# A two-half selective-scan block: output projection, second softplus and row norm moved

## The chip, the cores and the metric

The kernel runs on one core of a Trainium2 chip. Time is device time in microseconds (us) of one execution. Engines are named as in the profile: PE is TensorE's matrix multiply and PEld its weight load, DVE is VectorE, ACT ScalarE, POOL GpSimd, SP the engine that issues most transfers. The engines run side by side and wait for each other on semaphores; each runs its own instructions strictly in the order written.

## The reference, cut to what matters

Four sequences (batches) of 512 tokens with 128 channels pass a Mamba block with a mixture of experts, a feed-forward block, an attention and a feed-forward block. The change touches the Mamba block alone and the norm behind it:

```
xi, z = split(x @ in_proj_w)                 # 256 channels each
xi    = silu(causal_conv(xi) + conv_b)
dbc   = xi @ x_proj_w                        # 64 dt columns, 16 B, 16 C
delta = softplus(dbc[:, :64] @ dt_proj_w + dt_proj_b)
for n in 16 states:                          # scan over the 512 tokens
    h = exp(delta * A[n]) * h + (delta * xi) * B[n]
    y += h * C[n]
y = (y + D_skip * xi) * silu(z)
r = residual + y @ out_proj_w
h2 = r * rsqrt(mean(r * r) + eps) * w2       # then router, top 2 of 8 experts
```

## The kernel before, in words

Channels lie on the 128 partitions (256 channels are CT = 2 tiles) and tokens along the free dimension. The four batches are worked in two halves h = 0, 1 of HB = 2 batches each (c = 0, 1). In each batch the NS = 16 states are numbered on through g = 16 * (2h + c) + n, so the first half has states 0 to 31, the second 32 to 63.

**A state's work.** For each g, ScalarE writes the two decays `exp(delta * A)` into PSUM banks 6 and 7 (`decay`, L1061), each behind the scan of the state before that reads the same bank. GpSimd forms dBx (L850) from dx = delta * xc (L840 for c = 0, L855 for c = 1) and a row of B that SP has spread over all partitions, up to three states ahead. VectorE scans each tile (`scan`, L1387) and weighs the state by its row of C (`weigh`, L1397), for which ScalarE has copied that row into a bank (`copy_c`, L1057). Some states (1, 3, 6, 8, 11, 13 of a batch, in the last batch only 5 and 10) are weighed by GpSimd (L862) and have neither `weigh` nor `copy_c`. TensorE sums y in banks 0 and 1 by products with the identity (`ysum`). VectorE's order is scan(g, 0), weigh(g - 1), scan(g, 1). At the end of a batch `gate` multiplies by silu(z).

**The start of a half.** TensorE: `x_proj` of a batch (two products of 512 columns) and, once ScalarE has copied the result to SBUF (`row_copy`, L980), `dt_proj` (two more, banks 2, 3 for c = 0 and 4, 5 for c = 1). SP stores the copied B and C rows to DRAM and spreads them from there. ScalarE makes the softplus: `relu_abs` (Abs and Relu of each tile, L985 and L986) and `exp_log` (Exp, Ln over both tiles, L990 and L991). VectorE adds the two parts (`form_delta`, L1340), which sets the semaphore `s_dl` for GpSimd's dx and ScalarE's decays. In the first half the order is, on ScalarE, both row copies, the table load, then softplus of batch 0 and of batch 1, and on TensorE both x products, then both dt products. The scans start after both.

**The end of the first half.** `out_proj(0)` projects the gated y of the first half (32 matmul records, banks 0 and 1). It stands last in the second half's `inputs_1`, after both dt products. VectorE then adds it to the residual (`add_residual`, L1347), takes the moments for the norm, and GpSimd raises them to the power -1/2. This stands between form_delta(2) and form_delta(3), so ahead of all scans of the second half. `h2_norm(0)` multiplies the eight 128x128 tiles of the first half by their factors on VectorE (L1364), after the scans of state 35; TensorE transposes them at g = 36, ScalarE copies them out with w2 at g = 38 (`moe_input`, L957), then come router (39), logits (41), top (42), exp (43), second top part (44), rank (45) and slots (47), all woven between states by the table `ROUTE_AT`. From state 48 on GpSimd sends one `scatter` (L827) of normalised rows behind each dBx, sixteen in all. Similar tables (`COPY_AT`, `PREP_AT`) weave other copies into the first half.

## Time and profile before

| | us |
|---|---|
| median of 3 runs | 712.5 (711.13 to 716.41) |
| the profiled execution | 713.09 |
| its span in the trace | 711.1 |
| mean granted TensorE clock | 0.932 |
| busy: PE, DVE, ACT, POOL | 564.9, 495.1, 386.8, 329.6 |

The scans of the first half run from 48 to 147 us, those of the second from 175 to 291 us. Then come the mixture of experts with the first feed-forward block worked in, and the attention. A busy time counts instructions of an engine, not whether anything waits for them. In the timelines a row with "x8" is eight instructions of one kind that follow each other, with the time from the first one's start to the last one's end; in brackets stands the idle time of the engine before it and who ended it. PEclk is the granted clock of TensorE as a share of 2.4 GHz.

### The profile page before, as it was taken

What the parts mean: (1) busy time and instruction counts of PE and PEld (TensorE: products, weight loads), DVE (VectorE), ACT (ScalarE), POOL (GpSimd) and SP (SyncE); (2) the same over time, 40 slices, a digit from 0 to 9 for tenths busy, and PEclk for the clock granted to TensorE, in tenths of its full rate; (3) what the DMA queues carried; (4) which work ended last, traced back from release to release, by engine and by line L of the source; (5) the groups of instructions that cost most, each with busy time, mean ns of one, the idle gap of its engine ahead of it and who ended that gap; (6) DMA issues with size and microseconds to landing.
All of it is one profiled execution on the core that took longest, in us unless ns stands there. A gap on an engine that the chain in (4) does not pass through costs nothing.

```text
span 711.1 us, 11057 instructions
## 1 busy us (share of the span) xinstructions
PE 564.9 (79%) x3447; PEld 356.1 (50%) x3447; DVE 495.1 (70%) x1304; ACT 386.8 (54%) x610; POOL 329.6 (46%) x287
## 2 busy tenths in 40 slices
PE   3939789584585766688999899966789989989887
PEld 1314333232241222387999799932545545545366
DVE  5649999976999998634533565388787778887052
ACT  1586655575364445366766556623256566566741
POOL 5259989815788799232678332433012103112010
PEclk9978999988688988999999999976999999999999
DMA  5836555404566566030114200422103003000001
GB/s 148 282 124 189 152 177 157 154 26 152 178 179 205 170 166 167 18 88 12 46 54 120 86 20 24 116 82 77 39 2 105 10 3 107 3 3 1 2 16 46
DMA packets 50523, 65.91 MB, mean 93 GB/s; under 512 B 7730, under 2 KB 29250, under 8 KB 50210
## 3 DMA queue, kind: packets, MB, share of 16 engines
q1 hardware_dynamic: 45122, 59.27, 28.8%
q0 software_dynamic: 2496, 5.15, 2.0%
q10 hardware_dynamic: 2848, 0.78, 0.5%
q8 instruction: 29, 0.48, 0.3%
q14 instruction: 28, 0.23, 0.1%
HBM read 47.46 MB, written 9.52 MB: 80 GB/s over the span
## 4 chain that ended last, share of the span: by engine, by line
PE 32%; DVE 9%; issue 8%; POOL 5%; ACT 4%; ACTq 1%; DMA 0%; POOLq 0%; DVEq 0%
PE ps L1594 29%; DVE arena L1514 3%; POOL moe_out L835 2%; ACT arena L1129 2%; POOL moe_rows L827 1%; PE ps L1891 1%; DVE x L1449 1%; DVE nb L1228 1%; DVE stats L1215 1%; POOL arena L878 1%; ACT r L1129 1%; PE ps L1898 1%; ACT arena L1137 1%; ACT arena L1149 0%; ACTq L1119 0%
## 5 line engine op out<-in xcount | busy, mean ns | idle before, releaser
L1594 PE MATMUL ps<-arena 128*128 128x128 f32 (+11 forms) x2150 | 326.0, 328 | 41.1 <-DVE arena L1514 17.5
L1594 PEld LDWEIGHTS ps<-arena 128*128 128x128 f32 (+2 forms) x2150 | 207.4, 158 | 126.8 <-issue 55.6
L1594 PE MATMUL ps<-arena,ident 128*128 128x512 f32 x256 | 137.7, 681 | 67.2 <-DVE arena L1397 67.1
L1387 DVE TENSOR_TENSOR_SCAN arena<-ps,arena 128x512 f32<-128x512 f32 x128 | 149.0, 1205 | 7.8 <-ACT ps L1061 4.2
L1061 ACT ACTIVATE ps<-arena 128x512 f32<-128x512 f32 x128 | 87.7, 691 | 91.7 <-DVE arena L1387 91.5
L850 POOL TENSOR_TENSOR arena<-arena 128x1024 f32<-128x1024 f32 x64 | 127.1, 2004 | 7.2 <-DVE arena L1387 6.6
L1514 DVE CUSTOM_DVE_ANT_0 arena<-ps,cmask 128x128 f32<-128x128 f32 (+3 forms) x256 | 111.5, 487 | 26.4 <-PE ps L1594 26.0
L1594 PEld LDWEIGHTS ps<-arena,ident 128*128 128x128 f32 x256 | 52.8, 217 | 147.2 <-DVE arena L1397 91.8
L835 POOL DMA_INDIRECT moe_out<-arena,xT x46 | 44.9, 976 | 69.9 <-DVE arena L1538 57.4
L1129 ACT ACTIVATE arena<-ps 128x1024 f32<-128x1024 f32 (+3 forms) x86 | 57.1, 709 | 36.0 <-PE ps L1594 35.6
L1568 DVE TENSOR_TENSOR arena<-arena,ps 128x512 f32<-128x512 f32 x46 | 31.6, 687 | 63.9 <-PE ps L1594 46.5
L1175 ACT COPY arena<-arena 128x1024 f32 x46 | 48.2, 1047 | 23.6 <-issue 14.0
L807 POOL TENSOR_TENSOR small<-small,neghalf 128x4 f32<-128x4 f32 (+1 forms) x14 | 15.6, 1114 | 89.2 <-DVE small L1465 73.9
L1397 DVE TENSOR_TENSOR arena<-arena,ps 128x1024 f32<-128x1024 f32 x44 | 52.6, 1195 | 0.2
L862 POOL TENSOR_TENSOR arena<-arena 128x1024 f32<-128x1024 f32 x20 | 47.2, 2359 | 11.2 <-DVE arena L1387 10.5
L1185 ACT ACTIVATE arena<-ps 128x512 f32<-128x512 f32 x52 | 31.1, 598 | 24.0 <-PE ps L1594 22.5
L891 POOL TENSOR_TENSOR x<-x,arena 128x128 f32<-128x128 f32 x16 | 7.4, 461 | 67.4 <-DVE arena L1527 67.2
L827 POOL DMA_INDIRECT moe_rows<-nb,xT x32 | 32.2, 1008 | 13.3 <-issue 7.0
L1129 ACT ACTIVATE r<-ps 128x512 f32<-128x512 f32 (+3 forms) x42 | 27.8, 701 | 17.1 <-PE ps L1594 16.7
L1594 PE MATMUL ps<-kmask,identb 128*128 128x128 bf16 x256 | 35.1, 219 | 0.0
L1548 DVE TENSOR_TENSOR arena<-arena,ps 128x512 f32<-128x512 f32 x18 | 12.3, 684 | 27.1 <-ACT arena L1149 27.0
L1594 PEld LDWEIGHTS ps<-kmask,identb 128*128 128x128 bf16 x256 | 23.7, 98 | 12.4
(198 smaller groups left out, 621.3 us busy)
## 6 DMA issues: line engine op xcount, KB each, us to landing
arena<-bc_rows SPq DMA_DIRECT2D x128, 256.0 KB, 3.8
arena<-arena SPq DMA_DIRECT2D x64, 64.0 KB
arena<-arena SPq DMA_DIRECT2D x28, 128.0 KB, 2.5
moe_rows<-arena SPq DMA_DIRECT2D x2, 1495.0 KB, 11.7
arena<-moe_rows SPq DMA_DIRECT2D x8, 325.0 KB, 4.7
arena<-in_L_attn_a_Wg SPq DMA_DIRECT2D x8, 256.0 KB, 4.5
arena<-in_L_attn_a_Wu SPq DMA_DIRECT2D x8, 256.0 KB, 5.0
arena<-moe_out SPq DMA_DIRECT2D x4, 512.0 KB, 4.9
```

The lines of the kernel that those rows point to most:

```text
L827: G.indirect_dma_start(moe_rows[h], bass.IndirectOffsetOnAxis(ap=slotu[:, h, k, t:t + 1], axis=0), nbr[:, t // TB, t % TB, :], None).then_ ...
L835: G.indirect_dma_start(moe_out[h], bass.IndirectOffsetOnAxis(ap=target[:, h, k:k + 1], axis=0), yb[:, i % YR, :], None).then_inc(s_yst[i % ...
L850: G.tensor_tensor(dBx[:, g % RING, :, :], dx[:, :, cs], bs[:, g % BS, :].unsqueeze(1).to_broadcast([P, CT, L]), ALU.mult).then_inc(s_dbx, 1)
L862: G.tensor_tensor(hC[:, k % SUMS, :, :], hst[:, p % STATES, :, :], cs_rows[:, p % CS, :].unsqueeze(1).to_broadcast([P, CT, L]), ALU.mult). ...
L1061: S.activation(bank(6 + e), delta[:, e, c * L:c * L + L], ACT.Exp, scale=aneg[:, e, n:n + 1]).then_inc(s_da, 1)
L1129: S.activation(pts[c % 3][:, 2 * q:2 * q + 2, kt * P:L], ps[:, 2 * q:2 * q + 2, kt * P:L], ACT.Exp).then_inc(s_ex, 1)
L1175: S.copy(wst[:, i % 2, :, :].rearrange("p g f -> p (g f)"), wgu[:, bass.ds(expert, 1), :, :].rearrange("p o g f -> p (o g f)")).then_inc(s ...
L1387: V.tensor_tensor_scan(hst[:, g % STATES, e, :], bank(6 + e), dBx[:, g % RING, e, :], 0.0, ALU.mult, ALU.add).then_inc(s_scan, 1)
L1397: V.tensor_tensor(hC[:, k % SUMS, :, :], hst[:, g % STATES, :, :], bank(2 + dve_count(g) % 2).unsqueeze(1).to_broadcast([P, CT, L]), ALU.m ...
L1514: last = V.tensor_tensor_reduce(out=junk[:, m % 2, col:col + w], in0=ps[:, 4 + m % 2, col:col + w], in1=cmask[:, L - w:L], scale=-1.0, sca ...
L1568: V.tensor_tensor(hs[:, i % 2, :], sg[:, m % 2, :], bank(2 + m % 2), ALU.mult).then_inc(s_hm, 1)
L1594: return T.matmul(o, l, rr, start=start, stop=stop)
```

## The change

Seven edits, all at the two starts of the halves and at the routing of the first half:

- TensorE, first half: dt_proj(0, c) follows x_proj(0, c) batch by batch.
- TensorE, second half: out_proj(0) stands behind dt_proj(1, 0), ahead of x_proj(1, 1).
- ScalarE, both halves: row copy, Abs and Relu, Exp and Ln of batch 1 stand behind the decays and the C copy of the half's first state.
- VectorE, both halves: form_delta of batch 1 stands behind the scans of the half's first state; the weighing of that state waits for it.
- VectorE, second half: add_residual(0) stands ahead of form_delta(2), the moments behind it, and both ahead of the first scan.
- ScalarE has the first half's norm (`norm_h2`), four tiles behind state 35 and four behind state 36.
- The rest of the routing is one state later, and so are the scatters, with two behind the last state.

```diff
-        ROUTE_AT = {"h2norm": first_1 + 3, "h2turn": first_1 + 4, "input": first_1 + 6, "router": first_1 + 7,
+        NORM_AT = (first_1 + 3, first_1 + 4)
+        ROUTE_AT = {"h2turn": first_1 + 5, "input": first_1 + 7, "router": first_1 + 8,
...
-                        j = c * NS + n - NS
-                        if h and 0 <= j < 2 * TH:
+                        j = c * NS + n - NS - 1
+                        if h and 0 <= j < 2 * TH - 1:
                             scatter(0, j // 2, j % 2)
+                        if h and j == 2 * TH - 2:
+                            scatter(0, TH - 1, 1)
...
+            def norm_h2(c):
+
+                act.wait_ge(s_rstd, 3)
+                for j in range(TB):
+                    t = TB * c + j
+                    last = S.activation(nb[:, c, j, :], r[:, t, :], ACT.Copy, scale=small[:, 2, t:t + 1])
+                last.then_inc(s_h2, 1)
...
-                for c in range(HB):
-                    row_copy(0, c)
+                row_copy(0, 0)
                 S.preload_act_table_set("natural_log_exp_and_others")
-                for c in range(HB):
-                    relu_abs(0, c)
-                    exp_log(c)
+                relu_abs(0, 0)
+                exp_log(0)
...
                 relu_abs(1, 0)
-                row_copy(1, 1)
                 exp_log(0)
-                relu_abs(1, 1)
-                exp_log(1)
...
+                        if c == n == 0:
+                            row_copy(h, 1)
+                            relu_abs(h, 1)
+                            exp_log(1)
+                        if g in NORM_AT:
+                            norm_h2(g - NORM_AT[0])
...
-                    for b in range(HB):
-                        form_delta(b)
+                    form_delta(0)
                 else:
+                    add_residual(0)
                     form_delta(HB)
-                    add_residual(0)
-                    form_delta(HB + 1)
+                    residual_moments(0)
...
+                    if g == state_of(HB * h, 0):
+                        dve.wait_ge(s_dl, HB * h + HB)
...
-                        if g == ROUTE_AT["h2norm"]:
-                            h2_norm(0, count["var"])
+                        if c == n == 0:
+                            form_delta(HB * h + 1)
...
                     x_proj(0, c)
-                for c in range(HB):
                     dt_proj(0, c)
...
                 dt_proj(1, 0)
+                out_proj(0)
                 pe.wait_ge(s_xc, 2 * HB + 4)
                 pe.wait_ge(s_zc, 2 * HB)
                 x_proj(1, 1)
                 dt_proj(1, 1)
-                out_proj(0)
```

The order of instructions, first on ScalarE at the start of the first half, before (L980 is the row copy, L985 and L986 are Abs and Relu, L990 and L991 Exp and Ln, L1061 the decays, L1057 the C copy):

```order
L980 COPY arena<-ps 96x512 [waits x_proj_done] x2
L1012 ACT_TABLE_LOAD
L985 ACTIVATE arena<-ps,arena 128x512 [waits dt_proj_done]
...
L990 ACTIVATE arena<-arena 128x1024 [waits act_chain]
L991 ACTIVATE arena<-arena 128x1024 [waits act_chain]
L985 ACTIVATE arena<-ps,arena 128x512 [waits dt_proj_done]
...
L990 ACTIVATE arena<-arena 128x1024 [waits act_chain]
L991 ACTIVATE arena<-arena 128x1024 [waits act_chain]
L1061 ACTIVATE ps<-arena 128x512 [waits delta_ready]
```

and now (L991 is the row copy, L996 and L997 are Abs and Relu, L1001 and L1002 Exp and Ln, L1067 the decays, L1063 the C copy):

```order
L991 COPY arena<-ps 96x512 [waits x_proj_done]
L1022 ACT_TABLE_LOAD
L996 ACTIVATE arena<-ps,arena 128x512 [waits dt_proj_done]
...
L1001 ACTIVATE arena<-arena 128x1024 [waits act_chain]
L1002 ACTIVATE arena<-arena 128x1024 [waits act_chain]
L1067 ACTIVATE ps<-arena 128x512 [waits delta_ready]
L1067 ACTIVATE ps<-arena 128x512
L1063 COPY ps<-arena 128x512 [waits c_row_spread0]
L991 COPY arena<-ps 96x512 [waits x_proj_done]
L996 ACTIVATE arena<-ps,arena 128x512 [waits dt_proj_done]
...
L1002 ACTIVATE arena<-arena 128x1024 [waits act_chain]
L1067 ACTIVATE ps<-arena 128x512 [waits scan_done] x4
```

The second row copy and softplus have moved behind the first state's decays and C copy; the row copy and the dt product that answers it now stand between them and that softplus.

VectorE at the start of the second half, before (L1340 is the delta add, L1347 the residual add, L1215 the first step of the moments, L1387 the scan, L1397 the weighing):

```order
L1340 TENSOR_TENSOR arena<-ps,arena 128x2x512 [waits softplus_log_ready]
L1347 TENSOR_TENSOR r<-ps,r 128x512 [waits out_proj_done] x2
L1215 BN_STATS stats<-r 128x6 [waits residual_ready]
...
L1340 TENSOR_TENSOR arena<-ps,arena 128x2x512 [waits softplus_log_ready]
L1387 SCALAR_TENSOR_TENSOR arena<-ps,arena 128x512 [waits hC_on_pool_ready,dBx_ready,dA_ready]
```

and now (L1352 is the delta add, L1359 the residual add, L1227 the moments, L1400 the scan, L1412 the weighing):

```order
L1359 TENSOR_TENSOR r<-ps,r 128x512 [waits out_proj_done] x2
L1352 TENSOR_TENSOR arena<-ps,arena 128x2x512 [waits softplus_log_ready]
L1227 BN_STATS stats<-r 128x6 [waits residual_ready]
...
L1400 SCALAR_TENSOR_TENSOR arena<-ps,arena 128x512 [waits hC_on_pool_ready,dBx_ready,dA_ready]
L1400 SCALAR_TENSOR_TENSOR arena<-ps,arena 128x512 [waits dA_ready]
L1352 TENSOR_TENSOR arena<-ps,arena 128x2x512 [waits softplus_log_ready]
L1400 SCALAR_TENSOR_TENSOR arena<-ps,arena 128x512 [waits hC_ready,dBx_ready,dA_ready]
L1412 TENSOR_TENSOR arena<-arena,ps 128x1024 [waits y_summed,delta_ready,scan_done,c_row_copied]
```

The residual adds have gone ahead of the first delta add, and the second delta add has gone behind the scans of state 32.

ScalarE around states 35 to 39, now (L986 is the norm, L960 the copy with w2; before, no norm stood here and the copy with w2, L957, stood one state earlier, behind decays with no C copy):

```order
L1067 ACTIVATE ps<-arena 128x512 [waits scan_done] x2
L986 ACTIVATE nb<-r,small 128x128 [waits rstd_ready]
L986 ACTIVATE nb<-r,small 128x128 x3
L1067 ACTIVATE ps<-arena 128x512 [waits scan_done] x2
L1063 COPY ps<-arena 128x512 [waits hC_ready,c_row_spread0]
L986 ACTIVATE nb<-r,small 128x128 [waits rstd_ready]
L986 ACTIVATE nb<-r,small 128x128 x3
L1067 ACTIVATE ps<-arena 128x512 [waits scan_done] x2
L1063 COPY ps<-arena 128x512 [waits hC_ready,c_row_spread1]
L1067 ACTIVATE ps<-arena 128x512 [waits scan_done] x4
L1063 COPY ps<-arena 128x512 [waits hC_ready,c_row_spread0]
L960 ACTIVATE arena<-ps,w2c 128x512 [waits h2_transposed] x2
```

The norm stands behind the decays of state 35 and behind the C copy of state 36, the copy with w2 behind the C copy of state 39.

## Rows read from the trace of the kernel before

**Rows 1.** The chain that ended last, from 280 to 305 us: start us, us, what.
```profile
296.36 3.85 PE ps L1594 x32
```

**Rows 2.** Windows, two scan loops: busy (x) of PE, PEld, DVE, ACT, POOL; PEclk, DMA.
```profile
48.00:147.40 99.40, 78.20 (x178) 32.33 (x179) 95.21 (x84) 61.57 (x112) 90.91 (x44) 0.93 0.53 159
174.70:291.70 117.00, 76.94 (x160) 31.40 (x161) 112.57 (x143) 56.44 (x90) 95.57 (x55) 0.81 0.59 172
```

**Rows 3.** Timeline, VectorE, first half's start: start, us, engine, operation, [idle before <-releaser].
```profile
42.12 1.23 DVE L1340 TENSOR_TENSOR arena<-ps,arena 128x1024 f32<-128x1024 f32 x1 [9.29 <-ACT arena L991]
46.47 1.23 DVE L1340 TENSOR_TENSOR arena<-ps,arena 128x1024 f32<-128x1024 f32 x1 [3.12 <-ACT arena L991]
47.96 3.45 DVE L1387 TENSOR_TENSOR_SCAN arena<-ps,arena 128x512 f32<-128x512 f32 x3 [0.27 <-POOL arena L850]
```

**Rows 4.** Timeline, ScalarE, first half's start.
```profile
34.02 0.58 ACT L980 COPY arena<-ps 96x512 f32<-96x512 f32 x1 [0.44 <-PE ps L1594]
...
36.34 1.28 ACT L1012 ACT_TABLE_LOAD   x1
37.63 0.69 ACT L985 ACTIVATE arena<-ps,arena 128x512 f32<-128x512 f32 x1
```

**Rows 5.** Windows (us, PE busy (x), PEclk), then timeline, of TensorE at either clock.
```profile
41.00:42.00 1.00, 0.24 (x1) 1.00 0.15 55
...
45.00:46.00 1.00, 0.00 (x0) 0.50 0.00 0
...
158.00:159.00 1.00, 1.00 (x2) 0.50 0.71 160
...
155.51 1.98 PE L1594 MATMUL ps<-arena 64*128 64x512 f32 x4 [1.21 <-ACT arena L980]
...
179.27 3.78 PE L1594 MATMUL ps<-arena,ident 128*128 128x512 f32 x4 [9.05 <-DVE arena L1397]
```

**Rows 6.** Timeline, VectorE, second half's start.
```profile
163.73 1.23 DVE L1340 TENSOR_TENSOR arena<-ps,arena 128x1024 f32<-128x1024 f32 x1 [8.37 <-ACT arena L991]
...
167.50 0.69 DVE L1347 TENSOR_TENSOR r<-ps,r 128x512 f32<-128x512 f32 x1 [1.09 <-PE ps L1594]
168.22 1.65 DVE L1215 BATCH_NORM_STATS2 stats<-r 128x6 f32<-128x128 f32 x8
...
173.53 1.22 DVE L1340 TENSOR_TENSOR arena<-ps,arena 128x1024 f32<-128x1024 f32 x1
174.67 3.44 DVE L1387 TENSOR_TENSOR_SCAN arena<-ps,arena 128x512 f32<-128x512 f32 x3
```

**Rows 7.** Timeline, VectorE: the norm of the first half's rows, and the second half's.
```profile
185.86 6.22 DVE L1364 TENSOR_SCALAR nb<-r,small 128x128 f32<-128x128 f32 x8
...
308.97 1.65 DVE L1364 TENSOR_SCALAR nb<-r,small 128x128 f32<-128x128 f32 x8
```

**Rows 8.** Timeline, ScalarE, then VectorE, then ScalarE: copies between two states' decays.
```profile
75.73 0.42 ACT L967 CAST wuT<-ps 128x128 fp32r<-128x128 f32 x2
...
76.83 1.34 ACT L1061 ACTIVATE ps<-arena 128x512 f32<-128x512 f32 x2
...
77.60 1.22 DVE L1387 TENSOR_TENSOR_SCAN arena<-ps,arena 128x512 f32<-128x512 f32 x1 [0.81 <-ACT ps L1061]
...
198.35 1.25 ACT L957 ACTIVATE arena<-ps,w2c 128x512 f32<-128x512 f32 x2
```

**Rows 9.** Groups by form, ScalarE; then waits, 20 to 300 us (total us, times, longest).
```profile
L1162 ACT ACTIVATE arena<-ps,w2c 128x128 f32<-128x128 f32 x46 | 16.9, 367 | 19.6 <-PE ps L1781 19.6
...
ACT ps L1057 <- DMA arena<-bc_rows: 8.1, 10, 1.6
```

**Rows 10.** Timeline, GpSimd then VectorE, second half's last 16 states.
```profile
235.00 1.22 POOL L827 DMA_INDIRECT moe_rows<-nb,xT  x1 [4.07 <-DVE xT L1317]
...
288.01 1.01 POOL L827 DMA_INDIRECT moe_rows<-nb,xT  x1 [0.17 <-issue]
...
281.51 1.22 DVE L1387 TENSOR_TENSOR_SCAN arena<-ps,arena 128x512 f32<-128x512 f32 x1 [2.05 <-issue]
```

9 lines of the change are left out of this document (5 added, 4 removed).

## The prediction

> **What bounds the kernel now.** I read the windows over the two scan loops first. In the first loop VectorE is busy 95.2 of 99.4 us, in the second 112.6 of 117.0; ScalarE is busy about half of either, GpSimd 90.9 and 95.6 [rows 2]. So inside the loops time is won or lost on VectorE's stream, and a ScalarE instruction costs something only where it makes a decay late. Next I read the timelines at the two places where VectorE has no scan to do: the start of either half. In the first, VectorE waits 9.29 us for the softplus of batch 0, adds it (42.12), waits 3.12 us for batch 1's, adds that (46.47), and its first scan (47.96) waits 0.27 us more for GpSimd [rows 3]. In the second it waits 8.37 us, forms delta at 163.73, then takes the residual add, moments and the second delta (173.53) before its first scan at 174.67 [rows 6]. Last I read the chain from 280 us on: from the last scan it goes through the output projection (32 matmul records in 3.85 us, 296.36 to 300.21) into the mixture of experts [rows 1]. Everything after 300 us is unchanged and should shift as a block.
>
> **First half: the first scan earlier, the second state later.** Now TensorE runs batch 0's dt product ahead of batch 1's x product, and ScalarE has one row copy instead of two before its table load. The copy ends at 34.60, the load takes 1.28, so the first Abs can start at 35.9 instead of 37.63 [rows 4]. From that Abs to the delta add is 42.12 - 37.63 = 4.49 us, so the add comes at 40.4, and the first scan, 47.96 - 42.12 = 5.84 us behind it (GpSimd's two products), at 46.2: 1.7 us earlier. But state 1 now needs more. weigh of state 0 and the scans of state 1 stand behind the delta add of batch 1, and that behind ScalarE's: two decays (a pair takes 1.34 us [rows 8]), a C copy, the row copy of batch 1 (0.58), and a round trip to TensorE. The decays start when batch 0's delta is there, 41.65; the row copy ends at about 44.1. TensorE has by then stood still since about 38.5: batch 0's dt product from 34.65 and batch 1's x product, each as four records of 512 columns at 1.98 us [rows 5]. Before, its granted clock was still 1.00 in 41 to 42, where its work ended, and 0.50 (1.2 of 2.4 GHz) in 45 to 46 [rows 5]. The gap is now nearly 6 us, so I take the product at the lower level: four records of 512 columns took 1.98 us at the upper level and 3.78 at the lower [rows 5]. The two outputs are then there at 46.0 and 47.9; of the 4.49 us softplus, 1.14 precede the second Abs, so it ends at 47.9 + 3.35 = 51.25 and state 1's scan starts at 52.4. Before it started 2.24 us behind 47.96, at 50.2 (three scans in 3.45 us are 1.12 apart [rows 3]). **Term 1: +2.2 us**; at the upper clock 45.1 + 4.49 gives a scan at 50.8, +0.6.
>
> **Second half: the residual work into the wait.** out_proj(0) moves ahead of batch 1's x product on TensorE. It can start when dt_proj(1, 0) ends, 155.51 + 1.98 = 157.5 [rows 5]. The granted clock was 0.50 in 158 to 159 [rows 5], and TensorE's work up to 157.5 is the same, so I let the dip recur to 161: at 0.24 us a record (double of 3.85/32 [rows 1]) the first 16 records end at 161.3, the others at 163.2. VectorE adds the two residuals (0.69 each [rows 6]) at 161.3 and 163.2, and only then, being in order, forms batch 0's delta: at 163.9, no earlier than before (163.73 [rows 6]), though its softplus is ready at 161.3. GpSimd's products and the decays are queued behind that. Then come the moments: 173.53 - 168.22 = 5.3 us [rows 6], to 170.4; GpSimd's first dBx is there at 169.5. States of batch 0 start at 170.4. ScalarE meanwhile: decays at 165.1, C copy, row copy, done 167.4; dt product at the upper clock, first output 168.45, softplus to 172.95, delta to 174.15. Scan of state 33 at 174.15 against 174.67 + 2.24 = 176.9. **Term 2: -2.75 us.** With no clock dip in the output projection it is -4.5; with the dt product at the lower clock too, -0.9.
>
> **The norm.** The eight multiplications stop VectorE between two scans for 6.15 us (6.22, of which some 0.1 overlaps the next scan); the same eight take 1.65 us at 308.97 [rows 7]. The difference is that GpSimd is busy at 185.86. What leaves the path here is the 6.15 that it measures there. Is GpSimd then the next bound? It is busy 95.6 of 117.0 us in this loop [rows 2], so taking 6.2 us from the loop still leaves it over 15 us idle. **Term 3: -6.15 us.** The Trainium skill, SBUF — State Buffer, SBUF: two separate sides, says that a two-port VectorE form and GpSimd lock each other out for a whole instruction while ScalarE has ports of its own; the 6.22 against 1.65 us agree with it.
>
> **What ScalarE pays.** Its four multiplications for batch 0 fall behind state 35's decays, where no C copy stands; slack covers them. The other four come behind state 36's C copy, and state 35 is GpSimd's, so VectorE has no weighing to do between the scans that the next decay must catch. The same pattern stands in the first half: four small copies and one large one between 75.73 and 76.83 (1.10 us) made VectorE wait 0.81 [rows 8]. A 128x128 ACTIVATE of this kind takes 367 ns [rows 9]; started in a row I take 0.2 to 0.25 us apart, so four are 1.0 us and the stall 0.75. The two w2 copies (1.25 us [rows 8]) move from state 38, which had no C copy, to 39, which has one and follows a GpSimd state: by the same pattern 0.85; and they now wait for transposes that TensorE runs behind one more sum (3.78 us at the lower clock), so 0.95. **Term 4: +1.7 us**, 0.8 to 3. Bounds: nothing if the slack were as at the old places, twice 1.2 if none. The Trainium skill, ScalarE: Activation LUTs, What ACT_TABLE_LOAD costs, prices such an ACTIVATE at 386 ns with 93 ns of overlap; by it four take an estimated 1.27 us and the sum would be 0.25 us higher.
>
> **The rest.** The routing chain (logits, top, rank, slots) sits one state later throughout, and the first scatter too. GpSimd waited 4.07 us for the slots before it, then ran without a gap, and VectorE waited for it (2.05 us at 281.51 [rows 10]). It now starts one state of VectorE later (3.36 us) with one step of 3.2 us less to do before that point: **term 5: +0.1 us**. The sixteenth scatter moves behind GpSimd's last dBx; the fifteenth and sixteenth end about 290, the projection that gates the loads ends at 300.2 [rows 1, 10], so 10 us cover them; without that cover it would cost about 1 us. SP's store of batch 1's rows now waits for the later row copy, up to 44.1; behind it is the B row of state 3, which waits for GpSimd's first product (about 46) anyway. Sum: 2.2 - 2.75 - 6.15 + 1.7 + 0.1 = -4.9 us, from the profiled execution's 713.09 (span 711.1) to 708.2. That execution lies 0.6 above the median 712.5, so on its basis **707.6 us**, within 1% (about what a measurement of this kernel can tell from no change).
>
> **Rivals.**
> 1. *The clock stays up* at both places. Against it: the rows at 0.50; for it: the dip in the second half came while TensorE was at work, so a shift of 2 us may move it. Terms 1 and 2 become +0.6 and -4.5, which gives 704.2. Chance 0.2.
> 2. *Transfers and copies hold ScalarE.* Ten C copies waited 8.1 us in all for their row, the longest 1.6 [rows 9]. The pause of 6 us in which rows and expert weights arrived is gone, so three more such waits of about 1 us may surface as late decays: 710.6. Chance 0.18.
> 3. *GpSimd becomes the bound* when the pause goes. It decides if GpSimd's work from the norm to the slots is longer than VectorE's; then term 3 is worth nothing, and 2.2 - 2.75 + 1.7 + 0.1 = +1.25 gives 713.7: slower than before. The idle share in [rows 2] speaks against it. Chance 0.05.
> The forecast itself, 705.8 to 709.5, has 0.57.
>
> **How the numbers follow.** The range reaches from rival 1 to a little past rival 2: 704.0 to 711.2, which leaves out part of rival 1 and rival 3. Faster by over 1% is below 705.4: rival 1 and the forecast's edge, 0.25. Slower by over 1% (above 719.6) needs more than any rival gives: 0.02. The rest, 0.73, is within 1%.
>
> **What would show it.** In the changed profile: first scan at about 46.2 and VectorE waiting some 2.7 us for the Ln before batch 1's delta; the second dt product of the first half at clock 0.50. In the second half residual adds ahead of the delta, that delta near 166.1 (163.9 + 2.2), and state 33's scan near 176.4 (174.15 + 2.2). No VectorE tensor_scalar between states 35 and 36, and two waits for ScalarE of 0.7 to 1 us before states 37 and 40. The last projection near 295.5 instead of 300.2. I am wrong if the second delta of either half is not bound by ScalarE, if GpSimd ends the waits between 180 and 230 us, or if the block behind 300 us changes its length by over 1 us.

## The result

| us | before | changed |
|---|---|---|
| median of 22 runs each | 713.22 (711.13 to 716.41) | 710.55 (706.68 to 714.67) |
| ratio to before, 95% | | 0.9962 (0.9946 to 0.9977) |
| the profiled execution | 713.09 | 710.80 |
| its span | 711.1 | 709.0 |
| mean granted TensorE clock | 0.932 | 0.915 |
| busy: PE, DVE, ACT, POOL | 564.9, 495.1, 386.8, 329.6 | 576.2, 487.1, 389.4, 328.9 |

The change is worth 2.7 us by the medians (1.6 to 3.9 by the interval of the ratio), with 4.9 forecast. The times of all tables are us. PE is busy 11.3 us longer in this pair though its matmuls are the same: the mean granted clock was 0.915 against 0.932.

### The start of the first half

The timeline of the changed kernel, VectorE, 40 to 54 us (start, us, engine, line, operation, [idle before <-releaser]); it answers to [rows 3]:

```profile
40.79 1.23 DVE L1352 TENSOR_TENSOR arena<-ps,arena 128x1024 f32<-128x1024 f32 x1 [7.58 <-ACT arena L1002]
46.62 2.34 DVE L1400 TENSOR_TENSOR_SCAN arena<-ps,arena 128x512 f32<-128x512 f32 x2 [4.60 <-POOL arena L851]
51.58 1.23 DVE L1352 TENSOR_TENSOR arena<-ps,arena 128x1024 f32<-128x1024 f32 x1 [2.62 <-ACT arena L1002]
52.72 1.21 DVE L1400 TENSOR_TENSOR_SCAN arena<-ps,arena 128x512 f32<-128x512 f32 x1
```

ScalarE in the same place, and the clock of TensorE in two windows (us, busy (xinstructions) of PE, PEld, DVE, ACT, POOL, then PEclk, DMA share, GB/s); they answer to [rows 4, 5]:

```profile
43.80 0.57 ACT L991 COPY arena<-ps 96x512 f32<-96x512 f32 x1
46.54 0.69 ACT L996 ACTIVATE arena<-ps,arena 128x512 f32<-128x512 f32 x1 [2.16 <-PE ps L1610]
...
48.24 0.69 ACT L996 ACTIVATE arena<-ps,arena 128x512 f32<-128x512 f32 x1 [0.47 <-PE ps L1610]
...
42.00:43.00 1.00, 0.00 (x0) 0.00 (x0) 0.02 (x1) 0.95 (x2) 0.90 (x1) 0.61 0.00 0
43.00:52.00 9.00, 7.49 (x8) 2.33 (x8) 2.76 (x3) 6.34 (x10) 8.92 (x5) 0.50 0.38 105
```

The first scan comes 1.3 us earlier than before (46.62 against 47.96), state 1's scan 2.5 us later (52.72 against 50.2). What is late is batch 1's softplus: TensorE had stood still for 5.5 us when the row copy ended at 44.37, the clock had fallen to 0.50 in 42 to 43, and the dt product's two outputs let ScalarE start at 46.54 and, after 0.47 us more of waiting, at 48.24.

### The start of the second half

VectorE of the changed kernel, 161 to 176 us, beside [rows 6]; then the TensorE clock in two windows:

```profile
161.51 0.69 DVE L1359 TENSOR_TENSOR r<-ps,r 128x512 f32<-128x512 f32 x1 [4.14 <-PE ps L1610]
163.30 0.69 DVE L1359 TENSOR_TENSOR r<-ps,r 128x512 f32<-128x512 f32 x1 [1.09 <-PE ps L1610]
163.90 1.22 DVE L1352 TENSOR_TENSOR arena<-ps,arena 128x1024 f32<-128x1024 f32 x1
...
169.72 2.34 DVE L1400 TENSOR_TENSOR_SCAN arena<-ps,arena 128x512 f32<-128x512 f32 x2
173.75 1.23 DVE L1352 TENSOR_TENSOR arena<-ps,arena 128x1024 f32<-128x1024 f32 x1 [1.69 <-ACT arena L1002]
174.89 1.21 DVE L1400 TENSOR_TENSOR_SCAN arena<-ps,arena 128x512 f32<-128x512 f32 x1
...
158.00:162.00 4.00, 4.00 (x27) 2.96 (x26) 0.49 (x1) 3.99 (x6) 0.00 (x0) 1.00 0.44 120
...
169.00:173.00 4.00, 4.00 (x5) 1.17 (x4) 3.00 (x3) 3.50 (x6) 4.00 (x3) 0.50 0.47 116
```

The residual adds stand in what was a wait, as intended. The clock fell in another place than forecast: the projection (158 to 162) ran at 1.00, and in 169 to 173, where batch 1's dt product runs, it was 0.50. State 33's scan starts at 174.89. The first half ended 2.0 us later than before (the convolution's first multiplication on VectorE at 150.63, before at 148.63), so counted from there state 33 gained 4.0 us.

### What ScalarE's four copies and the routing cost

The eight norm copies on ScalarE (two rows), with the copy of a C row, the w2 copies and the logits copy further on:

```profile
181.24 1.26 ACT L986 ACTIVATE nb<-r,small 128x128 f32<-128x128 f32 x4
...
185.11 1.27 ACT L986 ACTIVATE nb<-r,small 128x128 f32<-128x128 f32 x4
...
195.44 0.59 ACT L1063 COPY ps<-arena 128x512 f32<-128x512 f32 x1 [0.89 <-DMA arena<-bc_rows]
195.97 1.26 ACT L960 ACTIVATE arena<-ps,w2c 128x512 f32<-128x512 f32 x2
...
207.27 0.21 ACT L974 COPY wtok<-ps 128x64 f32<-128x64 f32 x1 [2.49 <-PE ps L1610]
```

and the three scans on VectorE that waited for a decay behind them, with the router product on TensorE and its clock:

```profile
186.99 1.22 DVE L1400 TENSOR_TENSOR_SCAN arena<-ps,arena 128x512 f32<-128x512 f32 x1 [0.82 <-ACT ps L1067]
...
197.84 1.22 DVE L1400 TENSOR_TENSOR_SCAN arena<-ps,arena 128x512 f32<-128x512 f32 x1 [1.79 <-ACT ps L1067]
...
208.10 1.23 DVE L1400 TENSOR_TENSOR_SCAN arena<-ps,arena 128x512 f32<-128x512 f32 x1 [1.20 <-ACT ps L1067]
...
203.81 3.42 PE L1610 MATMUL ps<-rw,arena 128*128 128x8 f32 x16
...
200.00:208.00 8.00, 7.77 (x21) 5.26 (x22) 6.90 (x7) 3.75 (x8) 6.78 (x5) 0.50 0.64 216
```

Before, no scan between 174 and 238 us waited for ScalarE by over 0.3 us. Now they wait 0.82 + 1.79 + 1.20 = 3.81 us, where term 4 had 1.7. The second wait is a C row that came 0.89 us late by DMA, with 1.26 us of w2 copies behind it in front of the decays. In all six profiled executions of this kernel the second wait is 0.90 us plus the lateness of that row: the row is 0.25, 0.80, 0.86, 0.89, 0.91 or 1.61 us late, the scan waits 1.15, 1.70, 1.76, 1.79, 1.80 or 2.51 us. So the w2 copies by themselves cost the 0.9 that I had put down, and the row is what comes on top. Why the row is late no run shows.

The third wait I had costed at nothing: the copy of the logits now stands one state on, and waited 2.49 us for the router's sixteen products, which took 3.42 us at the lower clock; the decays are queued behind it. The other executions bear this out: in the second the clock was back at 1.00 from 202.3 us on, the products took 1.85 us and no scan waited there; in the five others they took 3.42 us and the scan waited 1.20 or 1.21.

A fourth wait for ScalarE, of 1.64 us at 257.83 (1.13 to 1.17 us at that state in the kernel before), costs nothing: from the first scatter to the last scan GpSimd sets the pace, with 0.30 us of idle time or less between its rows, and that stretch takes 52.2 us in all six.

### Behind 300 us

The chain that ended last, 280 to 300 us, of the changed kernel (start, us, what), for [rows 1]:

```profile
291.04 3.85 PE ps L1610 x32
```

The last projection ends at 294.89, before at 300.21: 5.3 us earlier, with 295.5 forecast. So the profiled execution has the whole forecast gain there, and 709.04 - 294.89 = 414.15 us behind it, against 410.86: 3.3 us were lost in a block that the change does not touch. Chains of both kernels run in step from there to 488 us; then two pieces in the attention differ. The changed kernel, and the kernel before at the second of them:

```profile
488.84 2.91 PE ps L1610 x10
...
509.05 4.59 PE ps L1610 x24
```

```profile
494.08 1.14 PE ps L1594 x8
...
512.73 2.96 PE ps L1594 x24
```

The clock in the changed kernel's windows is 0.50 in both pieces:

```profile
488.00:492.00 4.00, 3.77 (x14) 3.00 (x14) 2.07 (x11) 2.68 (x3) 2.22 (x3) 0.50 0.34 92
...
510.00:513.00 3.00, 3.00 (x16) 3.00 (x15) 0.00 (x0) 0.00 (x0) 0.00 (x0) 0.50 0.14 16
```

Two questions follow: which term was mis-sized, and whether the loss in the attention belongs to the change. The comparison of one profiled execution with one other can't answer either, so twelve of the runs below are the two kernels again. "Theory C" in the expectations is that the clock falls there by chance, whatever the kernel; theory B is that the change brings it.

### The profile page after: what moved, and what is told of

It is laid out like the page before. It is cut to its first block, busy times and chain, and to the rows that moved or that the text cites. A ratio compares the mean times of both kernels' runs of the same rounds, so it can differ in the third digit from the quotient of the medians.

```text
span 709.0 us, 11038 instructions
## 1 busy us (share of the span) xinstructions
PE 576.2 (81%) x3428; PEld 364.3 (51%) x3447; DVE 487.1 (69%) x1296; ACT 389.4 (55%) x618; POOL 328.9 (46%) x287
## 4 chain that ended last, share of the span: by engine, by line
PE 33%; DVE 9%; issue 7%; POOL 4%; ACT 4%; DMA 1%; ACTq 1%; POOLq 0%; another core or an unknown queue 0%; DVEq 0%; SPq 0%
PE ps L1610 30%; DVE arena L1530 3%; POOL moe_out L836 2%; ACT arena L1141 2%; POOL moe_rows L828 1%; DVE x L1465 1%; PE ps L1906 1%; DVE stats L1227 1%; POOL arena L881 1%; DVE nb L1240 1%; ACT r L1141 1%; PE ps L1913 1%; DMA arena<-moe_out 1%; ACT arena L1161 1%; ACT arena L1149 1%
## 5 line engine op out<-in xcount | busy, mean ns | idle before, releaser
L1610 PE MATMUL ps<-arena 128*128 128x128 f32 (+10 forms) x2131 | 328.8, 331 | 50.2 <-DVE arena L1530 17.9
L1610 PEld LDWEIGHTS ps<-arena 128*128 128x128 f32 (+2 forms) x2150 | 209.8, 159 | 135.9 <-issue 56.0
L1610 PE MATMUL ps<-arena,ident 128*128 128x512 f32 x256 | 140.2, 693 | 46.6 <-DVE arena L1412 46.5
L1400 DVE TENSOR_TENSOR_SCAN arena<-ps,arena 128x512 f32<-128x512 f32 x128 | 149.3, 1208 | 15.8 <-ACT ps L1067 8.0
L1067 ACT ACTIVATE ps<-arena 128x512 f32<-128x512 f32 x128 | 87.3, 690 | 81.2 <-DVE arena L1400 78.0
L1187 ACT COPY arena<-arena 128x1024 f32 x46 | 48.2, 1047 | 23.9 <-issue 14.5
L1412 DVE TENSOR_TENSOR arena<-arena,ps 128x1024 f32<-128x1024 f32 x44 | 52.7, 1198 | 0.2
L1063 ACT COPY ps<-arena 128x512 f32<-128x512 f32 x44 | 25.4, 577 | 8.6 <-DMA arena<-bc_rows 8.6
## 6 DMA issues: line engine op xcount, KB each, us to landing
arena<-bc_rows SPq DMA_DIRECT2D x128, 256.0 KB, 3.8
arena<-in_L_attn_a_Wg SPq DMA_DIRECT2D x8, 256.0 KB, 4.4
arena<-in_L_attn_a_Wu SPq DMA_DIRECT2D x8, 256.0 KB, 5.0
```

What stands on the lines that cost most here:

```text
L1067: S.activation(bank(6 + e), delta[:, e, c * L:c * L + L], ACT.Exp, scale=aneg[:, e, n:n + 1]).then_inc(s_da, 1)
L1187: S.copy(wst[:, i % 2, :, :].rearrange("p g f -> p (g f)"), wgu[:, bass.ds(expert, 1), :, :].rearrange("p o g f -> p (o g f)")).then_inc(s ...
L1400: V.tensor_tensor_scan(hst[:, g % STATES, e, :], bank(6 + e), dBx[:, g % RING, e, :], 0.0, ALU.mult, ALU.add).then_inc(s_scan, 1)
L1412: V.tensor_tensor(hC[:, k % SUMS, :, :], hst[:, g % STATES, :, :], bank(2 + dve_count(g) % 2).unsqueeze(1).to_broadcast([P, CT, L]), ALU.m ...
L1610: return T.matmul(o, l, rr, start=start, stop=stop)
```

## Experiments: one part at a time

Each diff is against the changed kernel. The first four runs share one chip, with 713.31 us for the kernel before (29 runs).

**The first half's start as before.**

```diff
-                row_copy(0, 0)
+                for c in range(HB):
+                    row_copy(0, c)
...
-                        if c == n == 0:
+                        if h and c == n == 0:
                             row_copy(h, 1)
...
-                    form_delta(0)
+                    for b in range(HB):
+                        form_delta(b)
...
                     x_proj(0, c)
+                for c in range(HB):
                     dt_proj(0, c)
```

> The changed kernel with the start of the first half as it was before: both row copies and both softpluses ahead of the first scan, both x products ahead of the dt products. Theory A (terms add up): this undoes the loss that the trace of the changed kernel shows there (state 1's scan 52.72 instead of 50.2 us), so the last output projection ends 2.0 to 2.5 us earlier than in the changed kernel, at about 292.6, and the time is 2 to 2.5 us below the changed kernel's median of 710.6. Theory B (what is gained ahead of 300 us is given back behind it, because the block behind starts earlier): the projection ends as early, but the whole is within 0.7 us of the changed kernel.

Measured: 708.61 us, ratio 0.9922 (0.9904 to 0.9941), 6 runs. By the medians that is 1.8 us faster than the changed kernel on the same chip (710.42, ratio 0.9959), by the ratios 2.6. So the first half's edit costs time, about what was expected of it. The profiled execution does not show it at the projection, which ends at 295.1 and not at the expected 292.6: its first half started late, with the granted clock at 0.50 from 33.4 to 36.8 us, and its stretch from state 33 to the last scan took 111.7 us. The section on the repeated executions sorts this out.

**The norm on VectorE again.** The rest of the change stays; routing and scatters stand at their old states.

```diff
-        NORM_AT = (first_1 + 3, first_1 + 4)
+        NORM_AT = ()
+        ROUTE_AT = {"h2norm": first_1 + 3, "h2turn": first_1 + 4, "input": first_1 + 6, "router": first_1 + 7,
+                    "logits": first_1 + 9, "top_a": first_1 + 10, "exp": first_1 + 11, "top_b": first_1 + 12,
+                    "rank": first_1 + 13, "slots": first_1 + 15}
...
+                        if g == ROUTE_AT["h2norm"]:
+                            h2_norm(0, 3)
```

> The changed kernel with the norm of the first half's rows back on VectorE behind state 35, and with it the routing and the scatters at their old states. Theory A: VectorE has its 6.2 us again and loses the three waits for ScalarE and the router (0.82, 1.79 and 1.20 us at 187, 198 and 208 us), so the last projection ends 2.0 to 2.8 us later than in the changed kernel, at about 297.3, and the time is up by as much. If the forecast's price for ScalarE (1.7 us) had been right it would be 4.4 us later. Theory B: later by 2 to 3 us at the projection, but the whole within 1 us of the changed kernel.

Measured: 714.08 us, ratio 1.0000 (0.9981 to 1.0019), 12 runs: 3.7 us over the changed kernel. VectorE, where the norm stands:

```profile
186.48 6.22 DVE L1377 TENSOR_SCALAR nb<-r,small 128x128 f32<-128x128 f32 x8
```

The price of the norm on VectorE is what it was (6.22, as in [rows 7]). I had expected 2.0 to 2.8 us and got 3.7 by the medians; by the ratios (1.0000 against 0.9959) it is 2.9, and the intervals do not rule out the forecast's 6.15 - 1.7. The trace is sharper: from state 33's scan to the last scan it takes 113.52 us, as in the kernel before, against 110.5 on average in the changed kernel, so the norm's move with all that it brings is worth 3.0. Without the norm's move the change brings nothing.

**The second half's start as before.**

```diff
+                row_copy(1, 1)
                 exp_log(0)
+                relu_abs(1, 1)
+                exp_log(1)
...
                 else:
-                    add_residual(0)
                     form_delta(HB)
+                    add_residual(0)
                     residual_moments(0)
+                    form_delta(HB + 1)
...
                 dt_proj(1, 0)
-                out_proj(0)
                 pe.wait_ge(s_xc, 2 * HB + 4)
...
                 dt_proj(1, 1)
+                out_proj(0)
```

> The changed kernel with the start of the second half as it was before: output projection last on TensorE, residual work between the two delta adds, both softpluses ahead of the first scan. Theory A: the last projection ends 2.5 to 4 us later than in the changed kernel (2.75 was the forecast's term with the clock at its lower level during the projection, 4.0 is what the two traces show), and the time is up by as much, to about 713 to 714. Theory B: the whole stays within 1 us of the changed kernel's.

Measured: 711.92 us, ratio 0.9983 (0.9967 to 1.0000), 12 runs: 1.5 us over the changed kernel, with 2.5 to 4 expected. The intervals of the two overlap (0.9938 to 0.9980 for the changed kernel), so the sign is likely and the size is rough. In its profile state 33's scan comes 26.66 us behind the end of the first half; in the changed kernel this is 24.26 in the first profile and 24.85 on average, so on average the second half's edit is worth 1.8 there. Together the three parts give +1.8 - 3.7 - 1.5 = -3.4 us, with -2.9 measured for the whole.

**The changed kernel again, and the kernel before again** (the second in a later series on the same chip, like the three runs behind it, with 713.71 us for the kernel before, 20 runs).

> The changed kernel again, for a second profile and as the yardstick of the three others. Theory C (the block behind 300 us varies with where TensorE's clock falls, whatever the kernel): it was 410.9 us long before and 414.1 us in the changed kernel's first profile; a second profile gives another value, anywhere from 410 to 415. Theory B: about 414 again. The last projection ends within 1 us of 294.9 unless the clock falls elsewhere in the first 200 us, which can move it by up to 2 us.

> The kernel before again, for a second profile and as a null comparison. Theory C (the clock moves both parts from one execution to the next, whatever the kernel): the last projection does not end at 300.2 us again and the block behind it is not 410.9 us long again; so far five profiles of the changed kernel and its variants gave 412.0 to 414.2, so about 412.5 is expected here too, with the projection ending between 298.5 and 301. Theory B (the block behind is longer because of the change): 410.9 us again, within 0.5. The ratio is 1.000 within 0.002.

Measured: 710.42 us, ratio 0.9959 (0.9938 to 0.9980), and 712.33 us, ratio 0.9991 (0.9968 to 1.0015). The medians repeat. Behind 300 us the changed kernel's second profile has 412.0 us (414.15 in the first) and that of the kernel before 410.6 (410.86): the latter is what theory B had expected, and I had expected 412.5 by theory C. The profile of the kernel before does not repeat, however, at the place that term 2 was read from. Here it is beside [rows 6], with the clock windows at the same place of this run and then of the first profile:

```profile
162.24 1.23 DVE L1340 TENSOR_TENSOR arena<-ps,arena 128x1024 f32<-128x1024 f32 x1 [6.76 <-ACT arena L991]
...
173.17 3.44 DVE L1387 TENSOR_TENSOR_SCAN arena<-ps,arena 128x512 f32<-128x512 f32 x3
...
159.00:160.00 1.00, 0.49 (x2) 0.00 (x0) 0.00 (x0) 0.70 (x2) 0.00 (x0) 1.00 0.93 240
```

```profile
159.00:160.00 1.00, 1.00 (x3) 0.28 (x1) 0.00 (x0) 0.17 (x1) 0.00 (x0) 0.50 0.78 225
```

The same kernel has the clock at 1.00 there, forms delta 1.5 us earlier and has its scan at 173.17 instead of 174.67. The dip on which I built term 2 was a matter of that one execution.

**TensorE kept busy ahead of the late dt products.** Small products into a bank that is free then.

```diff
+            def keep_warm(n):
+                for _ in range(n):
+                    mm(ps[:, 4, 0:P], ident[:], opw[:, 0, :])
...
                     x_proj(0, c)
+                    if c:
+                        keep_warm(20)
                     dt_proj(0, c)
...
                 x_proj(1, 1)
+                keep_warm(9)
                 dt_proj(1, 1)
```

> The changed kernel with 20 small products (128x128, operands already there, result overwritten) on TensorE ahead of batch 1's dt product in the first half and 9 in the second, to fill the time in which it waits for the row copy. If the lower clock is what makes that product late (two outputs 1.7 us apart in both halves of the changed kernel's profile instead of about 1), the granted clock stays at 1.00 there, the product takes 2.0 us instead of 3.4 to 3.8, and state 1's and state 33's scans come about 1.5 us earlier each: time down by up to 3 us against the changed kernel. If it is the row copy and the softplus themselves, nothing changes (within 0.5 us).

Measured: 708.03 us, ratio 0.9904 (0.9871 to 0.9937), 6 runs. ScalarE in its second half, then the clock in both places:

```profile
169.81 0.69 ACT L996 ACTIVATE arena<-ps,arena 128x512 f32<-128x512 f32 x1 [1.21 <-PE ps L1610]
...
170.97 0.69 ACT L996 ACTIVATE arena<-ps,arena 128x512 f32<-128x512 f32 x1
...
44.00:48.00 4.00, 4.00 (x37) 3.88 (x36) 0.22 (x1) 2.33 (x4) 3.62 (x2) 1.00 0.10 23
...
168.00:171.00 3.00, 2.46 (x6) 0.97 (x6) 2.84 (x12) 1.79 (x5) 2.92 (x3) 1.00 0.09 22
```

The clock stays at 1.00 and the wait of 0.47 us ahead of the second Abs is gone. But in the first half the twenty products stand in front of the dt product and hold it: ScalarE waited 2.42 us for it, where the changed kernel waited 2.16. State 1's scan came at 54.63 in this profile, because the clock was low from 33 to 43 us already; in the two executions of the changed kernel with such an early fall it came at 54.09 and 54.39. State 33's scan came 24.00 us behind the end of the first half, against 24.26. So its profile shows 0.3 us in the second half and nothing in the first, where I had expected 1.5 us each. By the medians the kernel is 2.4 us better than the changed one, by the ratios (0.9904 against 0.9959) 3.9. I can't account for that from the trace; with 6 runs and an interval of 4.7 us part of it may be chance.

**Norm copies and routing copies in the gaps.** The second four norm copies go one state on, behind the C copy of state 37, whose scans follow a weighing. Turn, input and router go one state on too, so the w2 copies come to state 40, which has no C copy.

```diff
-        NORM_AT = (first_1 + 3, first_1 + 4)
-        ROUTE_AT = {"h2turn": first_1 + 5, "input": first_1 + 7, "router": first_1 + 8,
+        NORM_AT = (first_1 + 3, first_1 + 5)
+        ROUTE_AT = {"h2turn": first_1 + 6, "input": first_1 + 8, "router": first_1 + 9,
```

> The changed kernel with the second four tiles of the norm one state later (behind state 37, two scans that follow a weighing), the transposes behind it, and the two w2 copies at state 40, which has no C copy, with the router at 41. Theory A: the waits of VectorE for ScalarE of 0.82, 1.79 and 1.20 us in the changed kernel go, all but about 0.5 us, so the time is 3 us lower than the changed kernel's. Rival: the time is bound there by something else that then shows (the C rows' transfers, or the router), and less than 1.5 us comes.

Measured: 708.03 us, ratio 0.9914 (0.9885 to 0.9943), 6 runs: by the ratios (0.9914 against 0.9959) 3.2 us better than the changed kernel, by the medians 2.4. The waits that are left:

```profile
191.24 1.23 DVE L1400 TENSOR_TENSOR_SCAN arena<-ps,arena 128x512 f32<-128x512 f32 x1 [0.85 <-ACT ps L1067]
...
207.18 1.22 DVE L1400 TENSOR_TENSOR_SCAN arena<-ps,arena 128x512 f32<-128x512 f32 x1 [1.29 <-ACT ps L1067]
```

2.14 us instead of 3.81, where I had expected about 0.5 to be left. The wait at the w2 copies is gone; the one behind the norm copies has only moved to state 38, and the one behind the logits copy (state 43) is 1.29 though the router's products took 1.84 us there; in both places a C row came over 1 us late (1.07 and 1.05). From state 33's scan to the last scan it takes 109.05 us, the changed kernel 110.5 on average: that is the 1.4 us of it that the trace shows. ScalarE's price depends on which gap a copy stands in, and the sum over the waits ahead of the first scatter is where it is read.

**The best of these: copies in the gaps, first half as before.** Both diffs above in one kernel.

> The same placement of norm, copies and router as in e7, and the start of the first half as before the change (as in e1, which was 1.8 us under the changed kernel). If the parts add up: 4.5 to 5 us below the changed kernel, at about 706.

Measured: 706.80 us, ratio 0.9918 (0.9892 to 0.9944), 9 runs. Its median is the lowest of all and near the expected 706, but its ratio is that of the run before it, so by the times the two can't be told apart (in its profile the last projection ends at 291.26, in that run's at 294.46); against the changed kernel both are better by the ratios (0.9914 and 0.9918 against 0.9959), with intervals that just overlap. One wait of 1.23 us for ScalarE is left between state 33 and the first scatter (scan at 189.88), and the span of its profiled execution is 702.9.

## Experiments: the same two kernels, again and again

To tell the change from the execution, both kernels were profiled on more occasions, one execution each, without an edit. The chips of these runs take some 10 us longer in the mixture of experts, so whole times are compared only within a chip; the stretches ahead of 300 us and the attention agree between chips.

> The kernel before, one more profile. In its two profiles the block from the last expert input (456.8 and 454.3 us) to the end of the span was 254.3 and 254.9 us long; in seven of the eight profiles of the changed kernel and its variants it was 257.2 to 257.6, with a drop of TensorE's granted clock some 58 us behind the last expert input that the kernel before did not show. Theory C (where the clock falls in that block is chance, whatever the kernel): a further profile of the kernel before shows the drop and about 257 in more than half of the cases. Theory B (the change brings it): 254 to 255 again and no drop.

> As the look before: theory C wants about 257 us behind the last expert input in one or both of the two, theory B 254 to 255 in both.

> The changed kernel, a third profile. Theory C: the block behind the last expert input lies anywhere from 254 to 258 us; theory B: 257 to 257.6 again. The last projection ended at 294.9 and 293.5 in the two profiles so far; the spread over the first 300 us comes from the clock during the dt products and the output projection of the two starts, so 293 to 297.

> As the look before. With four profiles of either kernel the mean end of the last projection should be about 5 us earlier in the changed kernel if the sum of the forecast holds for the first 300 us, or about 3 if the difference of the medians (2.9 us) is already made there.

> The kernel before, once more. The stretch from the last expert input copy to the end took 254.3, 254.9, 254.8 and 257.2 us in its four profiled executions, and 254.8 to 257.5 in the changed kernel's four, the long value with a low-clock stretch some 57 us behind the copy. Theory C (where the clock falls in the attention is chance, with the same odds for both kernels): of the four looks of the kernel before that are taken now, about two or more show 257. Theory B (the change makes the fall likely): at most one of the four does. End of the first half near 148.6, state 33's scan 26.7 behind it.

> As the fifth look of the kernel before: theory C gives about two or more long attention parts (257 us) in four looks, theory B at most one.

> As the fifth look of the kernel before: theory C gives about two or more long attention parts (257 us) in four looks, theory B at most one.

> The changed kernel once more. Both theories: 33rd state's scan 24.3 us behind the end of the first half, last projection 3 to 5 us earlier than in the kernel before on the same chip. Theory B expects the attention part near 257 us in nearly every look of this kernel; theory C in some two of three.

> As the fifth look of the kernel before: theory C gives about two or more long attention parts (257 us) in four looks, theory B at most one.

> As the fifth look of the changed kernel: theory B expects the attention part near 257 us in nearly every look of this kernel, theory C in some two of three.

Lengths of the stretches, each from its first row in VectorE's timeline, the projection's row in the chain, and the last expert's input copy on ScalarE:

| execution | start to end of first half | from there to state 33's scan | from there to the last scan | last projection ends at | last expert input to the end | span |
|---|---|---|---|---|---|---|
| before, first | 148.63 | 28.28 | 113.57 | 300.21 | 254.3 | 711.1 |
| before, second | 148.75 | 26.66 | 113.50 | 298.65 | 254.9 | 709.2 |
| before, third | 147.90 | 26.66 | 113.50 | 297.80 | 254.8 | 719.8 |
| before, fourth | 149.19 | 26.67 | 113.51 | 299.11 | 257.3 | 724.2 |
| before, fifth | 147.42 | 26.66 | 113.49 | 297.30 | 257.5 | 723.0 |
| before, sixth | 147.27 | 26.65 | 113.50 | 297.16 | 257.5 | 725.2 |
| before, seventh | 149.30 | 26.66 | 113.57 | 299.26 | 255.3 | 723.2 |
| before, eighth | 149.48 | 26.66 | 113.51 | 299.39 | 256.0 | 724.6 |
| changed, first | 150.63 | 24.26 | 110.26 | 294.89 | 257.5 | 709.0 |
| changed, second | 149.75 | 24.39 | 109.63 | 293.51 | 257.2 | 705.5 |
| changed, third | 152.10 | 24.26 | 110.23 | 296.33 | 257.3 | 720.0 |
| changed, fourth | 149.39 | 26.09 | 112.30 | 297.52 | 254.8 | 719.5 |
| changed, fifth | 152.21 | 24.27 | 110.24 | 296.45 | 255.9 | 721.3 |
| changed, sixth | 149.15 | 25.83 | 110.23 | 294.95 | 256.0 | 720.2 |
| mean, before | 148.49 | 26.86 | 113.52 | 298.61 | 255.9 | |
| mean, changed | 150.54 | 24.85 | 110.48 | 295.61 | 256.5 | |
| difference | +2.05 | -2.01 | -3.04 | -3.00 | +0.5 | |

**The start of the first half.** It has two forms. In three executions of the kernel before (fourth, seventh, eighth) and in two of the changed one (third, fifth) the granted clock was 0.50 from 33.1 to 33.6 us on, and the first scan comes some 2 us later. Like with like, state 1's scan is at 50.2 to 50.9 us before and at 52.5 to 52.7 changed, and with the early fall at 52.2 to 52.3 and at 54.1 to 54.4. The change costs 2.0 to 2.1 us in either form. The run with the first half as before had the early fall too, and its state 1 at 52.03: 2.2 us ahead of the changed kernel in that form.

**The attention.** Three of eight executions of the kernel before take 257 us there and the other five 254.3 to 256.0; of the changed kernel three of six take 257 and three 254.8 to 256.0. The second of the two pieces, in the kernel before (its fifth execution) and then in the changed kernel (its fourth), has the value that the other kernel had in the first pair:

```profile
523.06 4.59 PE ps L1594 x24
```

```profile
521.12 2.96 PE ps L1610 x24
```

The first piece takes 2.91 us in that execution of the kernel before (1.14 in its first) and 1.14 and 1.15 us in the changed kernel's last two (2.91 in its first). So the long attention comes with both kernels, and the 3.3 us that the first pair seemed to lose behind 300 us is for the most part not the change's. That fits theory C, chance; after four executions of each it was 1 of 4 against 3 of 4 and seemed otherwise. Of the four of the kernel before that were taken last two are long, where theory B allowed one at most. Whether the odds differ somewhat can't be told from fourteen executions; the means differ by 0.5 us. The Trainium skill (TensorE: Matmul & The Clock Gate, Part 1: The HAM clock gate) says that the chip's look at TensorE's activity is not tied to the kernel, so that one kernel meets it at another phase in each run. The traces agree: the changed kernel had 1.00 in 158 to 162 us in its first execution and 0.57 in 158 to 161 in its fourth.

**The second half's start.** 26.66 us is what the kernel before takes in seven of eight; the first profile, with the dip at 158 to 161, is the exception. The changed kernel takes 24.3 in four of six and 25.8 and 26.1 in the others. These two had the dip in the projection, as I had forecast it. The fourth execution's window, and its residual add:

```profile
158.00:161.00 3.00, 3.00 (x15) 2.82 (x15) 0.00 (x0) 2.97 (x6) 0.00 (x0) 0.57 0.61 160
...
161.79 0.69 DVE L1359 TENSOR_TENSOR r<-ps,r 128x512 f32<-128x512 f32 x1 [5.67 <-PE ps L1610]
```

The wait for the projection is 5.67 us there and 4.14 without the dip.

**State 33 to the last scan.** The three waits for ScalarE add up to 3.81, 1.97, 3.78, 4.54, 3.83 and 3.75 us in the six executions of the changed kernel, 3.6 on average. Something else moves there as well: two small VectorE instructions of the routing, 128x64 each, stand beside GpSimd's work. In the kernel before they took 1.39 and 0.59 us; in the changed one 0.33 and 0.23 (four executions), 1.67 and 0.22 (one) or 0.34 and 1.54 (the fourth execution):

```profile
219.36 1.54 DVE L1293 TENSOR_TENSOR wtok<-wtok,m 128x64 f32<-128x64 f32 x1
```

That is 1.98 against 1.0 us on average, a gain of 1.0 that I had not counted. What sets their length can be read beside GpSimd's rows. Each of the long ones starts while a GpSimd product over 128x1024 runs and ends 0.1 us or less behind that product: this one at 220.90 with the product at 220.82, and in the first profile of the kernel before at 213.76 with the product at 213.68. So the price is what is left of GpSimd's product at that moment, up to 1.77 us here.

The account of the stretch: -6.15 (norm) + 3.6 (waits) - 1.0 (small instructions) + 0.16 (one state of 3.36 us more ahead of the slots, one scatter step of 3.2 us less behind them) = -3.4, with -3.04 measured; 0.35 us stays open.

## Why the prediction was right and wrong

| term | forecast | difference of the means over 14 executions |
|---|---|---|
| 1, first half | +2.2 | +2.05 |
| 2, second half | -2.75 | -2.01 |
| 3 to 5, norm, ScalarE, routing | -6.15 + 1.7 + 0.1 = -4.35 | -3.04 |
| sum at 300 us | -4.9 | -3.00 |
| behind 300 us | 0 | about +0.5, not told from chance |
| whole | -4.9 | -2.7 (medians) |

The failed step is term 4, with term 2's base beside it. Of the 1.9 us between -4.9 and -3.0, term 4 makes +1.9, term 2 +0.7, and the two small instructions -1.0. The standard error of the first three differences is 0.4 to 0.6 us.

**Term 1 was right**, size and mechanism: the dt product at the lower clock, outputs at 46.5 and 48.2 where the working had 46.0 and 47.9, state 1's scan at 52.7 where it had 52.4.

**Term 2 named the right limit and was 0.7 too large.** The second delta is bound by ScalarE in all six executions (waits of 1.5 to 1.9 us), as forecast. The step that failed is "so I let the dip recur to 161" (it recurred in two of six), and above all the base under it: I subtracted my time for the changed kernel from the one profile of the kernel before that has 28.3 us there, where 26.7 is the rule. My own 25.5 for the changed kernel (28.28 - 2.75) is not far from the measured 24.85. Two errors partly cancelled: the base 1.4 too high, the forecast 0.7 too slow. The signs that I named show the same: delta near 166.1 and state 33 near 176.4, measured 163.90 and 174.89.

**Term 3 was right**: from state 33's scan to state 36's it takes 15.09 us in the eight executions of the kernel before and 8.97 in the six of the changed one, 6.12 less; put back on VectorE, the norm takes 6.22 us again, and GpSimd did not become the bound there. Where it bounds, from the first scatter to the last scan, the stretch went from 55.4 to 52.2 us: it lost the one scatter step that term 5 had moved out of it.

**Term 4 is the main miss**: 1.7 forecast, 3.6 measured, beyond the upper bound of 3 that I had given it. Three steps failed. The four copies take 1.26 us, not "1.0": there the Trainium skill (ScalarE: Activation LUTs, What ACT_TABLE_LOAD costs) had the better figure, 1.27 by my own estimate from it. Yet that wait came out at 0.82, near the 0.75. At the w2 copies the 0.95 was measured as 1.15 to 2.5: 0.90 for the copies, and 0.25 to 1.61 for a late C row, which is rival 2's mechanism, one place of it. And the wait of 1.2 us behind the router stands in no term. The working followed the w2 copies to what they wait for on TensorE, but not the logits copy, which waits there in the same way a little later.

Against this miss of 1.9 stands the gain of 1.0 on the two small instructions, which no term has either.

**"Everything after 300 us is unchanged and should shift as a block" is right on average and wrong for a pair of profiles.** I had written that over 1 us there would prove me wrong; the first pair had 3.3. That bound was set without knowing how far the block varies in one and the same kernel, which is 3.2 us in the attention alone (254.3 to 257.5).

**The rivals.** Rival 1 was half true: in four of six executions the projection took no dip, but the dt products of batch 1 ran at the lower clock in either half of the first execution, a combination for which I had no price (I had the dip in the projection alone, in neither, and in both). Rival 2's price, 710.6, is what was measured, but that is luck: its mechanism holds for only part, one late row of about 0.9 us on average, not three, and the rest comes from term 2's base and the router's clock. Rival 3 did not occur.

## What to carry to other kernels

When work moves from the bounding engine to one with slack, list every instruction on the receiving engine that waits for something and stands ahead of what the bound needs, moved ones included, and price each with its releaser at the slower clock. Before a term is built on a clock level at one place, profile the same kernel again: here a dip worth 1.6 us was there in one execution of eight. And where parts of a change have opposite signs, take the losing one out: the first half's edit cost 2 us, and without it, and with the copies in free gaps, the kernel took 706.8 us instead of 710.5 (medians of different calls).

## What was not expected of the hardware

- The granted clock falls at other places from execution to execution of one kernel, also while TensorE is busy: 0.57 in 158 to 161 us with PE busy 3.00 of 3.00. In the stretches of the table that moved the kernel before by some 2 us in the first half's start, by 1.6 us in the second's and by up to 3.2 us in the attention.
- A 128x64 instruction with two operands on VectorE (a subtraction and a multiplication) took 0.22 to 0.34 us or 0.58 to 1.77 us. The long ones started while a GpSimd product ran and ended 0.1 us or less behind it. At the second half's moments one of three 128x8 instructions took 1.86 us in the changed kernel, in the same way (its end 169.66, the product's 169.63), and its two neighbours 0.18 and 0.17; in the kernel before the three took 0.89, 1.92 and 0.17.
